# A decoder layer on one core: loads and half of the block copies issued by GpSimd, two tiles projected together, dummy matmuls at the start

## What is computed

```
x = ln(x + attn(x))        # 32 query heads over 8 key/value heads, head width 32; the softmax runs over the
                           # head dimension of one token: scores = einsum('bsdh,bseh->bsde', q, k) / sqrt(32)
x = ln(x + quant(x) @ quant(ctx))                  # quant: x/s + z rounded, clipped to 0..255, back to float
h = relu(x @ up_w) ** 2                            # 1024 -> 2048
y = h @ down_w + ((x @ fc1_w) @ expert_w) * sum(top2(x @ gate_w)) @ fc2_w
x = ln(x + ln(y) * gamma + beta)
```

## Time and profile before

| | us |
|---|---|
| median of 3 runs | 630.72 (629.39 to 633.28) |
| profiled execution, its own time | 629.14 |
| its span in the trace | 627.30 |
| mean granted TensorE clock | 0.992 |

### The profile page before, as it was taken

The page is one execution under the profiler, slowest core; times in us unless marked ns, Lnnn a source line. Parts: engine busy times, 40 slices in busy tenths (PEclk is TensorE's granted clock), DMA queues, the critical chain, the costliest instruction groups (busy, mean ns, idle before and its releaser), DMA issues.

```text
span 627.3 us, 9388 instructions
## 1 busy us (share of the span) xinstructions
PE 593.6 (95%) x3728; PEld 476.8 (76%) x3728; DVE 382.1 (61%) x515; ACT 299.1 (48%) x384; POOL 123.9 (20%) x162
## 2 busy tenths in 40 slices
PE   2799999998999899999999999999999999999993
PEld 1687877666776688788888888888888888888882
DVE  4947898889854355335333331338864565749976
ACT  4556688896684544333333342114344333323824
POOL 2811355735442022422210000000000000021000
PEclk9999999998999999999999999999999999999998
DMA  9766675673663668779998774203433336089913
GB/s 335 286 186 187 183 203 167 170 259 106 194 203 135 241 239 317 263 274 344 315 344 314 252 253 121 77 1 101 135 91 86 94 99 235 1 275 328 293 55 124
DMA packets 82252, 123.61 MB, mean 197 GB/s; under 512 B 23840, under 2 KB 50720, under 8 KB 82208
## 3 DMA queue, kind: packets, MB, share of 16 engines
q1 hardware_dynamic: 74592, 94.95, 45.6%
q0 software_dynamic: 5168, 19.40, 9.3%
q10 hardware_dynamic: 2448, 8.65, 4.3%
HBM read 83.13 MB, written 35.65 MB: 189 GB/s over the span
## 4 chain that ended last, share of the span: by engine, by line
PE 65%; DVE 1%; ACT 0%; issue 0%; ACTq 0%
PE psum L1552 33%; PE psum L1611 30%; PE psum L1519 0%; PE psum L1528 0%; PE psum L1527 0%; PE psum L1545 0%; DVE ffn_lo L1959 0%; DVE ffn_lo L1948 0%; ACT hx L1714 0%; ACT ffn_lo L1724 0%; DVE stat_n L1940 0%; DVE ffn_lo L1933 0%; DVE x1T_lo L1809 0%; PE psum L1536 0%; ACT x1T_hi L1645 0%
## 5 line engine op out<-in xcount | busy, mean ns | idle before, releaser
L1813 DVE TENSOR_TENSOR u_lo<-u_raw,u_hi 128x1024 fp32r<-128x1024 f32 x18 | 24.7, 1373 | 73.7 <-ACT u_hi L1650 73.7
L1552 PE MATMUL psum<-x1T_hi,u_hi 128*128 128x512 f32 x160 | 62.9, 393 | 0.7 <-DVE x1T_lo L1809 0.7
L1552 PE MATMUL psum<-x1T_hi,u_lo 128*128 128x512 f32 x160 | 62.3, 389 | 0.0
L1552 PE MATMUL psum<-x1T_lo,u_hi 128*128 128x512 f32 x160 | 62.3, 389 | 0.0
L1611 PE MATMUL psum<-x2T_lo,x2T_hi 128*128 128x512 f32 x264 | 62.1, 389 | 0.0
L1611 PEld LDWEIGHTS psum<-x2T_lo,x2T_hi 128*128 128x128 f32 x264 | 49.6, 188 | 10.3
L1552 PE MATMUL psum<-x2T_hi,u_hi 128*128 128x512 f32 x144 | 56.5, 392 | 0.0
L1552 PE MATMUL psum<-x2T_lo,u_hi 128*128 128x512 f32 x144 | 56.1, 389 | 0.0
L1552 PE MATMUL psum<-x2T_hi,u_lo 128*128 128x512 f32 x144 | 56.0, 389 | 0.0
L2090 POOL DMA_DIRECT2D x1T_hi<-r_scratch x4 | 2.9, 713 | 243.9 <-PE psum L1611 243.9
L1611 PE MATMUL psum<-x1T_hi,x2T_hi 128*128 128x512 f32 x216 | 50.4, 389 | 0.0
(11 more groups left out here) (258 smaller groups left out, 1237.3 us busy)
## 6 DMA issues: line engine op xcount, KB each, us to landing
d_raw<-in_L_ffn_down_w_dram SPq DMA_DIRECT2D x20, 512.0 KB, 7.7
t_scratch<-d_raw SPq DMA_DIRECT2D x20, 512.0 KB, 5.1
d_raw<-t_scratch SPq DMA_DIRECT2D x20, 512.0 KB, 3.8
c_sb<-in_ctx_dram ACTq DMA_DIRECT2D x16, 512.0 KB, 3.9
u_raw<-in_L_ffn_up_w_dram SPq DMA_DIRECT2D x16, 512.0 KB, 5.2
r_scratch<-f1b SPq DMA_DIRECT2D x10, 512.0 KB, 4.4
r_scratch<-f2b SPq DMA_DIRECT2D x10, 512.0 KB, 3.1
x_sb<-in_x_dram SPq DMA_DIRECT2D x8, 512.0 KB, 5.8
```

Of the source, the lines that this page charges most:

```text
L1552: mm = pe.matmul(acc_b[:, product_index(m, b) % 4], s, v, start=(k == 0 and i == 0), stop=(k == KT - 1 and i == 2))
L1813: dve.tensor_tensor(u_lo[:, m % 2], u_raw[:, m % 2], u_hi[:, m % 2].bitcast(F32), ALU.subtract).then_inc(S["u_lo_done"], 1)
```

## The change

1. SP's `load_residual`, `load_expert`, `load_fc2` and blocks 4 to 7 of each `regroup` and `ungroup` go to POOL's queue. Every waiter on the blocks now waits for two semaphores.
2. `load_x(1)` goes ahead of weight chunk 4. The first two context loads wait until the last weight chunk has landed.
3. Tile 1 gets the accumulator of the cross product (`xa_ps`), and tiles 0 and 1 are contracted chunk by chunk, interleaved, as chunks become ready; `transpose_x(2)` stands in the middle of them, `scores(0)` behind half of tile 2.
4. 18 and 110 matmuls of 128 columns whose result nobody reads stand ahead of and behind `transpose_x(0)`.
5. All five orders are new. `cross(0)` goes from behind the projection of tile 5 to before it, and crosses 1 to 3 follow it forward. On DVE `quant_constants` stands between `prepare(6)` and `prepare(7)`, on ACT `split_w(7)` behind `ctx_a(0)`.
6. DVE's x2 norm (tiles 6 and 7) counts on its own semaphore, so that SP may store out of order.

```diff
+        qkv_of = lambda t: xa_ps if t == 1 else qkv_ps
+        SP_OUT = 4
+        SP_BLOCKS = 4
@@ SP
-                for n in range(NG):
+                for n in range(SP_BLOCKS):
                     sp.dma_start(pg[:, t % 2, n], qkv_sb[rows16(n), t % 2]).then_inc(pg_in[t % 2], 16)
...
             for k in range(KT):
                 load_w(k)
-            load_x(1)
+                if k == 3:
+                    load_x(1)
...
@@ PE
+            def contract(t, k):
+                st = [x[:, t % 2, k] for x in (xT_hi, xT_lo)]
+                for i in range(3):
+                    for c0, c1 in ((0, BANK), (BANK, QKV)):
+                        s, v = split_products(st, [w[:, k, c0:c1] for w in (w_hi, w_lo)])[i]
+                        mm = pe.matmul(qkv_of(t)[:, c0:c1], s, v, start=(k == 0 and i == 0), stop=(k == KT - 1 and i == 2))
+                return mm
+
+            def project_early(t, k):
+                if k == 0:
+                    pe.wait_ge(S["xT_lo_done"], t + 1)
+                pe.wait_ge(S["wq_lo_done"], k + 1)
+                pe.wait_ge(S["wkv_lo_done"], k + 1)
+                mm = contract(t, k)
+                if k == KT - 1:
+                    mm.then_inc(S["qkv_ready"], 1)
...
+            def warm(n):
+                pe.wait_ge(S["masks_done"], 3)
+                for _ in range(n):
+                    pe.matmul(sc_ps[:, 0:TQ].rearrange("p n d -> p (n d)"), so["ident_bf"][:], so["ident_bf"][:], start=True, stop=True)
...
+            warm(18)
             transpose_x(0)
-            project(0, 0)
+            warm(110)
             transpose_x(1)
-            project(0, 1)
-            project(1, 0)
-            project(1, 1)
+            project_early(0, 0)
+            project_early(0, 1)
+            project_early(1, 0)
+            project_early(0, 2)
+            project_early(0, 3)
+            project_early(1, 1)
+            project_early(1, 2)
+            project_early(1, 3)
             transpose_x(2)
+            project_early(0, 4)
+            project_early(0, 5)
+            project_early(1, 4)
+            project_early(0, 6)
+            project_early(0, 7)
+            project_early(1, 5)
+            project_early(1, 6)
+            project_early(1, 7)
+            project(2, 0)
             scores(0)
-            project(2, 0)
+            project(2, 1)
             values(0)
-            project(2, 1)
...
             values(2)
+            column_sums(0)
             scores(3)
+            transpose_q1(0)
             transpose_x(5)
-            column_sums(0)
+            cross(0)
             project(5, 0)
-            transpose_q1(0)
             values(3)
...
@@ ACT
+                if c < 2:
+                    act.wait_ge(wraw_in[KT - 1], 48)
                 act.dma_start(c_sb[:, c % 2], c_tiles[c]).then_inc(c_in[c % 2], 16)
...
@@ POOL
+            def regroup(t):
+                pool.wait_ge(S["qkv_evac"], t + 1)
+                if t >= 2:
+                    pool.wait_ge(S["scores_ready"], t - 1)
+                    pool.wait_ge(S["vT_done"], t - 1)
+                for n in range(SP_BLOCKS, NG):
+                    pool.dma_start(pg[:, t % 2, n], qkv_sb[rows16(n), t % 2]).then_inc(pgp_in[t % 2], 16)
+
+            def ungroup(t):
+                pool.wait_ge(S["o_done"], t + 1)
+                for n in range(SP_OUT, NG):
+                    pool.dma_start(o_tok(t)[rows16(n)], o_sb[:, t % 2, n]).then_inc(op_in[t % 2], 16)
...
             values_ones()
+            regroup(0)
             keys_diagonal(0)
+            regroup(1)
             values_diagonal(0)
+            load_residual(0)
             keys_diagonal(1)
+            ungroup(0)
             values_diagonal(1)
+            regroup(2)
+            load_residual(1)
+            load_residual(2)
             keys_diagonal(2)
```

More of the change, by code:

```diff
@@ L142, in attention_and_cross @@
         pg_in = [sem("pg_in0"), sem("pg_in1")]
+        pgp_in = so["pgp_in"]
         o_in = [sem("o_in0"), sem("o_in1")]
-        res_in = [sem(f"res_in{i}") for i in range(XR)]
+        op_in = so["op_in"]
+        res_in = so["res_in"]
         x2_st = so["x2_st"]
@@ L156, in attention_and_cross @@
         bias_in, quant_in = sem("bias_in"), sem("quant_in")
-        ex_in, fc2_in = sem("ex_in"), [sem(f"fc2_in{i}") for i in range(MT)]
+        ex_in, fc2_in = so["ex_in"], so["fc2_in"]
         block = ctx.enter_context(nc.Block())
@@ L482, in _ @@
             values(2)
+            column_sums(0)
             scores(3)
+            transpose_q1(0)
             transpose_x(5)
-            column_sums(0)
+            cross(0)
             project(5, 0)
-            transpose_q1(0)
             values(3)
+            transpose_q1(1)
+            scores(4)
+            transpose_x(6)
             project(5, 1)
-            transpose_x(6)
-            cross(0)
-            scores(4)
-            transpose_q1(1)
+            cross(1)
             project(6, 0)
+            values(4)
+            transpose_q1(2)
             project(6, 1)
-            cross(1)
-            values(4)
+            cross(2)
             scores(5)
-            transpose_q1(2)
+            transpose_q1(3)
             transpose_x(7)
-            cross(2)
+            cross(3)
+            scores(6)
             project(7, 0)
-            transpose_q1(3)
-            scores(6)
             project(7, 1)
-            cross(3)
             values(5)
@@ L682, in _ @@
             ctx_a(2)
[L683 removed]
+            keys_diagonal(0)
             ctx_b(2)
@@ L984, in _ @@
             prepare_lo(0)
+            xT_lo_out(0)
             prepare(2)
+            prepare(3)
             prepare_lo(1)
-            prepare(3)
+            prepare_lo(2)
             prepare(4)
-            prepare_lo(2)
+            xT_lo_out(1)
+            prepare_lo(3)
+            prepare_lo(4)
             prepare(5)
             prepare(6)
-            prepare_lo(3)
+            quant_constants()
             prepare(7)
-            prepare_lo(4)
             prepare_lo(5)
             prepare_lo(6)
+            ctx_magic(0)
             prepare_lo(7)
@@ L1214, in _ @@
             values_diagonal(3)
+            ungroup(2)
             pool.wait_ge(S["quant2_done"], 1)
+            row_term(0)
+            regroup(4)
             add_column_term(0)
+            add_column_term(1)
             keys_diagonal(4)
[L1218 removed]
+            load_residual(3)
+            row_term(1)
+            inverse_deviation_x1(2)
+            ungroup(3)
             values_diagonal(4)
[L1220 removed]
             inverse_deviation_x2(0)
[L1222 to L1223 removed]
+            add_column_term(2)
+            load_fc2(0)
+            regroup(5)
+            inverse_deviation_x1(3)
+            row_term(2)
+            load_residual(4)
+            ungroup(4)
             keys_diagonal(5)
[L1225 to L1228 removed]
+            regroup(6)
+            row_term(3)
             add_column_term(3)
             inverse_deviation_x2(1)
+            load_fc2(1)
+            keys_diagonal(6)
             values_diagonal(5)
             inverse_deviation_x2(2)
+            load_expert()
+            load_fc2(2)
+            values_diagonal(6)
             inverse_deviation_x1(4)
[L1234 to L1235 removed]
             inverse_deviation_x2(3)
+            regroup(7)
+            load_fc2(3)
+            ungroup(5)
             keys_diagonal(7)
+            load_residual(5)
+            row_term(4)
+            load_residual(6)
             add_column_term(4)
[L1239 removed]
+            ungroup(6)
             inverse_deviation_x1(5)
+            load_residual(7)
             values_diagonal(7)
[L1242 removed]
             inverse_deviation_x1(6)
             row_term(5)
+            add_column_term(5)
+            ungroup(7)
+            add_column_term(6)
             inverse_deviation_x2(4)
@@ L2152, in decoder @@
         so["u_in"] = [ctx.enter_context(nc.semaphore(f"u_in{i}")) for i in range(2)]
+        so["res_in"] = [ctx.enter_context(nc.semaphore(f"res_in{i}")) for i in range(XR)]
+        so["fc2_in"] = [ctx.enter_context(nc.semaphore(f"fc2_in{i}")) for i in range(MT)]
+        so["ex_in"] = ctx.enter_context(nc.semaphore("ex_in"))
+        so["pgp_in"] = [ctx.enter_context(nc.semaphore(f"pgp_in{i}")) for i in range(2)]
+        so["op_in"] = [ctx.enter_context(nc.semaphore(f"op_in{i}")) for i in range(2)]
         so["x2_st"] = [ctx.enter_context(nc.semaphore(f"x2_st{i}")) for i in range(XR)]
```

412 lines of the change are left out of this document (194 added, 218 removed).

## The result

The changed kernel takes 640.80 us (639.25 to 643.62) against 630.99 for the kernel before on the same chip (629.39 to 633.28): a ratio of 1.0167, 95% interval 1.0134 to 1.0199. It is 1.7% slower, where 629.2 us and no change were forecast. So the two profiles differ by 14.5 us where the medians differ by 9.8.

A forecast was written before the change was run, and what follows sets the result against it. TensorE, busy 95% of the span, was taken as the bound, with only its arrival at stage two (207.73 us) movable. 629.14 + 1.7 - 4.7 + 1.5 = 627.6 us, plus 1.6 to the median: 629.2; range 621 to 641.

The forecast's parts named there:

- The start: Stage one up to transpose_x(3): between 0.8 us won and 1.7 us lost, taken as 1.7 us lost.
- Tile 2's gate: transpose_x(2) waits for its tile's load until 29.2 us (28.5 to 30.0), with some 4 us idle before it.
- T3: Start of transpose_x(3), 52.52 us in the kernel before; forecast at 51.7 at full clock, 54.3 with a slow restart.
- The other gate: Chunk 5's low part on VectorE stands behind quant_constants, whose last constant lands at 28.5 us, nearly when tile 2 does.
- +1.7: The start's term: transpose_x(3) 1.7 us later, since a restart at 1.2 GHz after idle time costs 2.6 us.
- New waits 1.5, bounds 0 and 4.7: Rest of stage one: new waits around the four earlier crosses cost 1.5 us, at least 0, at most 4.7.
- -4.7 + 1.5: Rest of stage one: at most 4.7 us of old waits and slow scores removed, 1.5 us of new waits added.
- GpSimd at nothing: GpSimd's 48 new issues from 80 to 160 us, 0.6 us each, were taken to cost no time.
- at 90% it keeps up: GpSimd busy 72 of 80 us from 80 to 160 still keeps up; threshold 0.76 us an issue.
- rival (d): GpSimd becomes the bound in stage one, its issues held up: 643.8 us at most, about 640; chance 0.17.
- The fillers at nothing: The 128 dummy matmuls at the start, at most 13.7 us within TensorE's waiting time, cost nothing and don't help the clock.
- Stage two untouched: From 207.73 us on TensorE runs almost alone, in pieces of 130.57 and 190.41 us, which the change leaves as is.

The follow-up runs named there:

- a2: The changed kernel with GpSimd's second column-term addition moved three steps back, behind the key masks: 635.91 us, ratio 1.0111 to the kernel before.
- a3: The changed kernel with VectorE's low part of tile 5 put ahead of the long context operation: 638.78 us, ratio 1.0147.
- b4: a2 with two more moves: GpSimd's regroup(5) ahead of an addition and an fc2 load, TensorE's transpose_x2(0) behind w2_product(1): 637.10 us, ratio 1.0101.
- c1: The changed kernel with VectorE's quant_constants and ctx_magic(0) moved behind prepare(7), the last low parts and the biases, and ScalarE's split_w(7) ahead of ctx_a(0): 647.44 us, ratio 1.0271.
- c3: b2 with the new start mended: tile 2 and constants loaded ahead of bias rows, constants' step behind the weights, transpose_x(2) behind project_early(0, 7): 632.81 us, ratio 1.0047.
- d1: c3 with ScalarE's xT_hi_out(2) ahead of ctx_a(0), and VectorE's constants behind the last weight part and xT_lo_out(2) ahead of ctx_magic(0): 632.65 us, ratio 1.0030.
- e2: d1 with ScalarE's keys_diagonal(0) ahead of ctx_a(2): 630.49 us, ratio 1.0001.
- b3: The kernel before with only the new start, the first 50 us of the changed kernel; the rest and all issuing as before: 637.60 us, ratio 1.0112.
- b1: The kernel before in its own orders, with GpSimd issuing all residual, expert and fc2 loads and half of the block copies: 636.36 us, ratio 1.0097.
- b2: The kernel before with only half of the block copies issued by GpSimd, the large loads staying on SP: 628.66 us, ratio 0.9981.
- d4: b1 with the expert and fc2 loads back on SP, the residual loads still on GpSimd: 630.69 us, ratio 1.0012.
- d2: d1 without the 128 filling matmuls: 631.71 us, ratio 1.0029.
- d3: The changed kernel without its 128 filling matmuls, nothing else changed: 641.25 us, ratio 1.0166.
- e1: The changed kernel with its first 50 us put back as in the kernel before, issuing and later orders as changed: 643.41 us, ratio 1.0213.
- c4: b1 with GpSimd's inverse_deviation_x2(3) moved ahead of values_diagonal(6), regroup(7) and ungroup(5): 639.54 us, ratio 1.0139.

## Why the prediction was wrong

**The start** was right in kind. Tile 2's gate was forecast at 29.2 with some 4 us of idle time; it is 30.55 with 4.20, and pairs 0.64 us apart behind it. T3 was put at 54.3 and came at 56.13, in a2, a3 and b4, whose start is the same, at 53.71 to 55.37: the size is as good as one profile can tell. Part of that is luck. The gate opened 1.35 us later than forecast, and the slow clock held five pairs (31.44 to 34.78) and not nine, so that half of tile 2 was done at 45.7 us, where the forecast has it too (43.1 + 2.6). Behind that the scores wait 1.25 us instead of 0.7, `values(0)` 0.54 instead of 1, and 1.48 us for o_sb were not in the sum: `values(0)` now stands directly before `transpose_x(3)`, which has to wait until its result is evacuated. The other gate, the constants, was named as "nearly one time" and then left; c1, c3, d1 and e2 show that opening it only hands the wait on until four more places are in step. The forecast saw +1.7, this profile has +3.6, and in the old orders the new start costs 1.1% (b3).

**"New waits 1.5, bounds 0 and 4.7"** is the step that failed by most. The waits of 0.56, 0.37 and 1.79 us for k_bd, q1T and q are gone or no longer than 0.5, as said; in their place stand 4.38, 2.01 and 2.33 us, 8.7 together where the sum had 1.5 and its bound was 4.7, each with slow clock behind it. The rest was forecast 3.2 us shorter (-4.7 + 1.5) and is 11.0 longer. I had priced new waits by their usual size in the old order, though a new order's waits come from pairs of steps that it puts together. The dearest pair could be read from the diff: two additions back to back on GpSimd beside a VectorE operation of the kind that one addition had already held.

**GpSimd at nothing** is the second step that failed. It was right in the mean price of an issue (0.54 to 0.69 us in the groups by line; 0.6 taken from the earlier trace rows) and wrong in the test, "at 90% it keeps up". In the kernel after its windows show 60.64 us of 80, 76%. In b1, where its new work is alone, it is 69.48 us, 87% and so what was forecast, and b1 loses 7.7 us to b2: in 120 to 160 us it is 96% busy, and small results come late behind issues. A share under 100% doesn't clear an engine that works in order. So rival (d), priced at 0.76 us an issue, had the engine right and the mechanism wrong.

Single issues were held up, and the means hide it. The Trainium skill, SBUF — State Buffer, Who interferes with whom, has this too (GpSimd is kept from writing descriptors while such an operation of VectorE runs), and the trace agrees. Of the kernel after's 81 in stage one 76 take 0.52 to 0.70 us, two 0.96 and 1.02. Both of these lie beside a whole VectorE tensor_scalar, as the first of the four here, which alone takes 0.96 us:

```profile
129.61 2.54 POOL L1197 DMA_DIRECT2D pg<-qkv_sb  x4 [0.82 <-DVE qkv_sb L982]
```

```profile
129.76 0.69 DVE L969 TENSOR_SCALAR f2b<-f2b 128x1024 f32<-128x1024 f32 x1 [0.44 <-ACT f2b L583]
```

b1 has seven of 0.77 us or more, 2.3 us over the usual 0.55 in all; b2 and d4, which lose nothing, have 2 us of it as well. That is not the loss.

**The fillers at nothing** was right in time (d2, d3). **Stage two untouched** was right. The terms summed to -1.5 us at the begin of stage two, where the profile has +14.6. That 640.80 us lies just inside the range of 621 to 641 is owed to the half of rival (d) that it took in, and (d)'s mechanism isn't what happened.

What stays open: how the 1.7% divide in the kernel after itself. On the orders of before the new start costs 1.1% (b3) and the new issuing 1.0% (b1), together no less than the whole; what the new order behind T3 adds or wins back is then within the noise of the four times. Inside the kernel after the additions are worth about 3.5 us (a2); the rest of the new order and the late large loads could not be separated there (b4, e1).

## To carry to other kernels

When a change moves steps in orders written by hand, read each new neighbour for what it waits for, and list what stands behind it; a removed wait is worth little unless the next step in every engine's order has its input. Look at the share of an in-order engine stretch by stretch before giving it large loads beside late small results: here 96% over 40 us cost 7.7 us, though over 80 us it was 87%. And test such a change by its parts on the old orders: here the half of the copies was harmless, and what surrounded it was not.

## What the runs showed of the hardware

One VectorE tensor_scalar of 0.68 us took 3.19 beside one GpSimd tensor_tensor of 2.42 us and 5.82 beside two of together 4.69 us: it ended 0.65 and 1.0 us after them, about its own length, as if it had stood still until both were over. One GpSimd DMA issue of usually 0.55 us took up to 1.03 us beside such a VectorE operation (b1, at 117). Copies of 48 KB issued by GpSimd landed in 2.1 to 2.3 us at 88.33 and in 4.3 to 6.7 at 118.93, right behind a 512 KB load on its queue.

The clock does not answer to one wait alike: in the kernel before a wait of 2.18 us left the pairs 0.36 us apart, while in b1 the pairs behind a wait of 2.18 us at 32.91, for the same step in the same order, were 0.64 apart. The executions had parted before that. First the kernel before, then b1:

```profile
20.83 0.62 PE L341 MATMUL psum<-w_hi,xT_hi 128*128 128x512 f32 x2 [0.50 <-DVE w_lo L893]
```

```profile
22.83 1.01 PE L314 MATMUL psum<-w_hi,xT_hi 128*128 128x512 f32 x2 [2.84 <-DVE w_lo L871]
32.91 0.96 PE L314 MATMUL psum<-w_hi,xT_hi 128*128 128x512 f32 x2 [2.18 <-DVE xT_lo L947]
```

In b1 VectorE waited longer for its weight chunks to land (0.50, 0.47 and 0.81 us, against 0.39 and 0.35 in the kernel before), so TensorE stood 2.84 us and not 0.50, and was slow behind it. That makes 2.1 of the 3.6 us by which T3 is late, the slow pairs behind 32.91 the rest. What ran before isn't the whole answer either: b2 was slow from 24.97 to 27.04 too and kept a pace of 0.35 behind the same wait. T3 in b1, c4 and e1, whose start is in the old order, is at 56.0 to 56.3, in d4 at 52.63. A single profile of this kernel's start is thus uncertain by 3.6 us.
